# Value blocks projected in the attention's output banks, and the reciprocal rms row fetched by two DMAs

## What is computed

```python
# layer 0, 8 heads of 64 channels
hn = group_norm(x, gn1_scale, gn1_bias)                       # 32 groups
q, k, v = split(einsum('bchw,oc->bohw', hn, w_qkv) + b_qkv)   # per head
wgt = softmax(einsum('bct,bcs->bts', q * scale, k * scale))   # 1024 x 1024
a = einsum('bts,bcs->bct', wgt, v)
x = x + group_norm(einsum('bchw,oc->bohw', a, w_proj) + b_proj, gn2_scale, gn2_bias)
# layer 1, one head of 512 channels
qkv = einsum('oc,bcn->bon', w_qkv, x)            # weight-normed
rms = sqrt(mean(square(qkv), axis=1, keepdims=True)) + 0.0001
q, k, v = split(qkv / rms, 3, axis=1)
attn = softmax(einsum('bci,bcj->bij', q, k) * C ** -0.5)
h = einsum('bij,bcj->bci', attn, v)
out = (x + einsum('oc,bcn->bon', w_out, h)) * 2 ** -0.5
```

## Time and profile before

| | |
|---|---|
| runs | 3520.0, 3522.6, 3522.65 us |
| profiled execution | 3520.63 us |
| its span | 3518.8 us |
| TensorE's mean granted clock | 0.999 of full speed |

### The profile page before, as it was taken

The page is one execution under the profiler, slowest core; times in us unless marked ns, Lnnn a source line. Parts: engine busy times, 40 slices in busy tenths (PEclk is TensorE's granted clock), DMA queues, the critical chain, the costliest instruction groups (busy, mean ns, idle before and its releaser), DMA issues.

```text
span 3518.8 us, 52658 instructions
## 1 busy us (share of the span) xinstructions
PE 3457.8 (98%) x17360; PEld 2832.2 (80%) x17360; DVE 2077.7 (59%) x3388; ACT 1826.7 (52%) x3074; POOL 1086.0 (31%) x947
## 2 busy tenths in 40 slices
PE   7999999999999999999999999999999999999999
PEld 4788888878888788887878878788787887888878
DVE  4677436773378634786347854488444884457742
ACT  3677226862278522784237832388223882247822
POOL 0344203441045410453104531145211452124521
PEclk9999999999999999999999999999999999999999
DMA  8522214312234113331143220342213422142210
GB/s 312 156 53 61 92 54 127 85 37 84 82 99 97 66 43 103 89 86 72 37 121 89 68 84 34 112 97 61 84 37 110 95 61 84 43 137 62 61 48 24
DMA packets 63519, 294.41 MB, mean 84 GB/s; under 512 B 9200, under 2 KB 9456, under 8 KB 52464
## 3 DMA queue, kind: packets, MB, share of 16 engines
q1 hardware_dynamic: 63216, 290.65, 28.0%
HBM read 158.49 MB, written 31.46 MB: 54 GB/s over the span
## 4 chain that ended last, share of the span: by engine, by line
PE 85%; issue 6%; DVE 3%; ACT 2%; DMA 2%; POOL 2%; SPq 0%; ACTq 0%; DVEq 0%; POOLq 0%
PE big L430 28%; PE tps L529 14%; PE big L556 12%; PE ops L542 12%; PE ops L702 10%; PE big L626 6%; PE ops L430 1%; DVE XA L1252 1%; ACT PB L828 1%; PE big L594 1%; DMA d_m<-PT 1%; DMA d_u<-ST 1%; POOL XA L968 1%; DVE HL L1257 0%; DVE small L1180 0%
## 5 line engine op out<-in xcount | busy, mean ns | idle before, releaser
L958 POOL TENSOR_SCALAR PB<-PB,small 128x1024 f32<-128x1024 f32 x576 | 650.2, 1129 | 1304.4 <-DVE small L1186 1293.6
L834 ACT ACTIVATE PT<-tps 128x512 fp32r<-128x512 f32 x1088 | 601.7, 597 | 250.9 <-PE tps L529 247.8
L1191 DVE TENSOR_TENSOR PT<-tps,PT 128x512 fp32r<-128x512 f32 x1088 | 693.8, 679 | 39.0 <-ACT PT L834 38.6
L1180 DVE TENSOR_REDUCE small<-big 128x1 f32<-128x1024 f32 x512 | 625.1, 1221 | 63.7 <-PE big L556 60.3
L529 PEld LDWEIGHTS tps<-ident,PB 128*128 128x128 f32 x4608 | 526.8, 140 | 125.5 <-DVE PT L1191 56.2
L529 PE MATMUL tps<-ident,PB 128*128 128x128 f32 x4608 | 618.0, 275 | 9.0 <-DVE PT L1191 6.1
L828 ACT ACTIVATE PB<-big,small 128x1024 f32<-128x1024 f32 x512 | 572.6, 1118 | 74.3 <-DVE small L1180 71.3
L542 PE MATMUL ops<-PT,VT 128*128 128x512 f32 x2048 | 599.2, 414 | 0.0
L556 PE MATMUL big<-ST 128*128 128x512 f32 x2048 | 555.0, 393 | 12.3 <-ACT PB L828 11.2
L556 PEld LDWEIGHTS big<-ST 128*128 128x128 f32 x2048 | 381.9, 188 | 103.2 <-ACT PB L828 19.8
L542 PEld LDWEIGHTS ops<-PT,VT 128*128 128x128 f32 x2048 | 346.1, 189 | 47.4 <-DVE PT L1191 5.0
(11 more groups left out here) (158 smaller groups left out, 4652.2 us busy)
## 6 DMA issues: line engine op xcount, KB each, us to landing
ST<-ST SPq DMA_DIRECT2D x384, 256.0 KB, 5.0
W<-d_qk SPq DMA_DIRECT2D x32, 1024.0 KB, 5.3
XA<-in_x SPq DMA_DIRECT2D x8, 2048.0 KB, 7.7
X<-in_x SPq DMA_DIRECT2D x8, 2048.0 KB, 10.5
W<-d_wp SPq DMA_DIRECT2D x8, 2048.0 KB, 11.6
W<-d_g SPq DMA_DIRECT2D x8, 2048.0 KB, 11.9
W<-d_m SPq DMA_DIRECT2D x8, 2048.0 KB, 7.9
W<-d_u SPq DMA_DIRECT2D x8, 2048.0 KB, 10.2
```

The source lines that it names most:

```text
L834: act_fn(pt_slot(u, s)[:, 0, :], tps[n % 2][:], ACT.Copy).then_inc(s_pt_hi, 1)
L958: nc.gpsimd.tensor_scalar(PB[:, i, :], PB[:, i, :], rinv[:, i:i + 1], 1.0, ALU.mult, ALU.mult)\
L1180: V.tensor_reduce(negmax[:, i:i + 1], tile(("s", 4 * u + tb))[:], axis=AX.X, op=ALU.max, negate=True).then_inc(s_row_max, 1)
L1191: V.tensor_tensor(pt_slot(u, s)[:, 1, :], tps[n % 2][:], pt_slot(u, s)[:, 0, :].bitcast(f32), ALU.subtract).then_inc(s_pt_ready, 1)
```

## The change

Two things are changed. The value blocks 4 to 7 are all projected in the `ops` banks, one in each of the attention steps 0 to 3; two `big` tiles instead of three are filled with values ahead of the attention. Blocks 6 and 7 use the banks of blocks 4 and 5 again and wait for VectorE to have read these. The low parts of the four blocks are made by VectorE one step later each, as before.

The reciprocal row is no longer made by TensorE. `rcol` is stored by SP into a DRAM tensor of 1024 numbers, element by element in position order, SP waits for that store, and loads the row from there into RB with all 128 partitions reading the same 4 KB. Both come in SP's queue after the load of W for the value products and ahead of the wait for `("y", 3)`. The identity products, the ones product and the copy are gone, and ScalarE waits for `rcol` itself.

```diff
 def last_values(step):
-    return {0: NT - 2, 3: NT - 1}.get(step)
+    return {0: 4, 1: 5, 2: 6, 3: 7}.get(step)
...
-BIG = [("qk", j) for j in range(4)] + [("v", i) for i in range(3)]
+BIG = [("qk", j) for j in range(4)] + [("v", i) for i in range(2)]
...
-BIG += [("y", 0), ("y", 1), ("y", 2), ("y", 3), ("u", 0), ("u", 1), ("u", 2), ("r", 0)]
+BIG += [("y", 0), ("y", 1), ("y", 2), ("y", 3), ("u", 0), ("u", 1), ("u", 2)]
...
+        d_r = nc.dram_tensor("d_r", [N], f32)
...
-                sp.wait_ge(s_v_full, b * 2 + 2)
+                sp.wait_ge(s_v_full, b * 4 + 4)
...
                 sp.dma_start(W[0][:].bitcast(f32), d_u[:]).then_inc(s_ld_u, 16)
+                sp.wait_ge(s_r_col, b + 1)
+                own_wait(sp)
+                sp.dma_start(d_r.ap().rearrange("(s p) -> p s", p=P), rcol, allow_slow_non_contiguous=True)\
+                  .then_inc(s_r_stored, 16)
+                sp.wait_ge(s_r_stored, b * 16 + 16)
+                own_wait(sp)
+                sp.dma_start(RB[:], d_r.ap().partition_broadcast(P)).then_inc(s_r_row, 16)
...
                 def project_last_v(s):
-                    if s == NT - 2:
+                    if s == 4:
                         pe.wait_ge(s_y_out, b * 8 + CREDIT)
+                    if s >= 6:
+                        pe.wait_ge(s_v_ready, b * 6 + s - 3)
...
-                for i in range(3):
+                for i in range(2):
                     project_v(i)
...
-                t = released(("r", 0))
-                pe.wait_ge(s_diag_ready, b + 1)
-                for half in range(2):
-                    cols = slice(HALF * half, HALF * half + HALF)
-                    last = mm(t[:, cols], ones[:], PB[:, 0, cols], start=True, stop=True)
-                last.then_inc(s_big_full, 1)
...
-                act.wait_ge(s_diag_ready, b + 1)
+                act.wait_ge(s_r_col, b + 1)
...
-                link(V.reciprocal(rcol, rms))
-                for s in range(NT):
-                    last = V.tensor_scalar(PB[:, 0, P * s:P * s + P], ident[:], rcol[:, s:s + 1], None, ALU.mult)
-                last.then_inc(s_diag_ready, 1)
+                V.reciprocal(rcol, rms).then_inc(s_r_col, 1)
...
-                dve.wait_ge(s_big_full, at(("r", 0)))
-                V.tensor_copy(RB[:], tile(("r", 0))[:]).then_inc(s_r_ready, 1)
...
-                        dve.wait_ge(s_r_ready, b + 1)
+                        dve.wait_ge(s_r_row, b * 16 + 16)
```

More of the change, by code:

```diff
@@ L74 @@
 BIG_BASE = SETUP_BIG
-DVE_LINKS = 18
+DVE_LINKS = 17
 SCALE0 = float(CH) ** -0.5
@@ L244, in build @@
         s_rms_done = sem("rms_done")
-        s_diag_ready = sem("diag_ready")
-        s_r_ready = sem("r_ready")
+        s_r_col = sem("r_col")
+        s_r_stored = sem("r_stored")
+        s_r_row = sem("r_row")
         s_y_ready = sem("y_ready")
@@ L486, in released @@
                         kind, k = (BIG_LAST if last_batch else BIG)[i - 2]
-                        reader, per = {"v": (s_v_ready, 5), "qk": (s_nat_ready, 16), "s": (s_exp_done, 72),
+                        reader, per = {"v": (s_v_ready, 6), "qk": (s_nat_ready, 16), "s": (s_exp_done, 72),
                                        "proj": (s_pr_ready, 4), "gna": (s_gn_var, GN_PER_BATCH),
                                        "gnb": (s_gn_veps, GN_PER_BATCH),
-                                       "g": (s_prod_ready, 4), "r": (s_r_ready, 1),
+                                       "g": (s_prod_ready, 4),
                                        "y": (s_y_ready, 4), "u": (s_vp_ready, 8), "s1": (s_s1_ready, 8)}[kind]
@@ L536, in values0 @@
                         if u == 0:
-                            pe.wait_ge(s_v_ready, b * 5 + 5)
+                            pe.wait_ge(s_v_ready, b * 6 + 6)
                         elif u > 1:
@@ L809, in last_v_hi @@
                 def last_v_hi(s):
-                    act.wait_ge(s_v_full, b * 2 + s - 5)
+                    act.wait_ge(s_v_full, b * 4 + s - 3)
                     act_fn(v_heads(s, s + 1)[:, :, 0:4:3, :], ops[s % 2][:].rearrange("p (q x d) -> p q x d", x=2, d=CH),
@@ L1162, in last_v_lo @@
                 def last_v_lo(s):
-                    dve.wait_ge(s_v_hi, b * 2 + s - 5)
+                    dve.wait_ge(s_v_hi, b * 4 + s - 3)
                     v = v_heads(s, s + 1)
```

## The result

The changed kernel takes 3500.6 us (median; 3499.7 to 3503.7 over four runs), the kernel before 3522.4 us in the runs beside it. The ratio is 0.9942, with a 95% interval of 0.9928 to 0.9957: 21.8 us less in the medians. The forecast was 3504.4 us. Between the two profiled executions, which are what the forecast's sum was made from, 19.2 us went (3501.4 against 3520.6), where the sum said 18.2.

What follows compares the result with a forecast made beforehand. TensorE, busy in 98% of the span, was taken as the bound. Terms -15.2 (row), -8.1 (early scores), +3.5 (batch 0) and +1.6 (clock) gave -18.2 us: 3504.4 us from the 3522.6 median, range 3499 to 3514.

Steps and rivals of the forecast that it cites:

- the forecast's sum: Whole kernel: -15.2 for the row, -8.1 for values, +3.5 and +1.6 in batch 0, together -18.2 us.
- The row's price: TensorE between value products u2 and u4: removing the ones product saves 1.90 us a batch, 15.2 us in all.
- the bank's wait: Before value product u3: a 0.68 us wait for a bank, included in the row's 1.90 us, would go.
- The two DMAs: Row's store and load on SP: together 4 to 31.5 us, taken as about 10, at no path cost.
- 35.6 us of cover: Time from when the reciprocal's store can go out to the first scaled maximum, which reads the row first.
- The early scores: Attention step 0 starts after 0.66 us idle for the sixth stacking copy; seven batches gain 1.16 us each, 8.1 us.
- the lead: Step 4 starts 1.16 us earlier, at 543.84 instead of 545.00, in seven batches.
- Batch 0: Late sixth copy leaves TensorE idle 6.5 us before step 0: +3.5 us, and +1.6 us for a slow clock.
- the two slow pieces: Stretches behind the 1.8 us idle time ahead of gram products, where the clock fell: 1.57 us each, two of eight batches.
- The rival of five or more slow pieces: Clock falls behind the idle time ahead of gram products in most batches: 3510 to 3514 us; chance 0.15.
- The third rival: Element store outlasts its cover, the scaled maximum waits, each microsecond costs eight: 3611 us at 0.6 us a piece; chance 0.03.
- The point of decision: Store and load together beyond 35.6 us delay the maximum; from 37.9 us on the kernel is slower than before.

Runs made afterwards that it cites:

- filled kernels: Seven unread matmuls a batch added in TensorE's idle time ahead of the third gram product: kernel before 3516.4, values only 3513.2, full change 3498.4 us.
- early copies: Full change, with the second pair's weight load behind the first head's six copies and its query copies sent before the key products: 3495.3 us.
- early copies with the matmuls: Kernel with the query copies sent early, plus seven unread matmuls a batch ahead of the third gram product: 3489.2 us.
- old kernel with the matmuls: Kernel before the change, plus seven unread matmuls a batch ahead of the third gram product: 3516.4 us.
- late row: Full change, with the row's store and load held back on SP until the last value product is full: 3567.7 us, ratio 1.0133.

## Why the prediction was right, and where its working was not

**The row's price.** Forecast 1.90 us a batch, measured 2.03 between batches of the kernel with the row alone, 1.90 between u2 and u4 (7.34 to 5.44), and 1.77 by the filled kernels with the 0.13 of the bank to add. The share of the bank's wait, which I put into the 1.90 without a number of its own, is 0.13 us; the 0.68 us idle time of the weight loads in the earlier trace rows was mostly hidden under the ones product. Right.

**The two DMAs.** The store was between the bounds, 9.2 us median and 11.7 in batch 0 (385.89 to 397.62), where I had taken 10 us for store and load together; with the load's 5.8 they make 15 to 17.5 us. Both lie within the 35.6 us of cover. The load behind them on SP went out at 398.13 and nobody waited for it. The Trainium skill's rule ("DMA: Bandwidth & Descriptors", "Rules for kernel authors": one descriptor per element) agrees with this trace: the packet counts above have one small packet for each number, and the 4 KB took over four times as long as a store of 256 KB. It cost nothing, since the end did not depend on it. One sentence of the prediction was wrong: the trace before did have pieces under 512 B. The load of `vec`, 48 floats on each of 128 partitions and so 192 B a piece, landed in 4.3 us:

```profile
vec<-in_vecs SPq DMA_DIRECT2D x1, 24.0 KB, 4.3
```

It would not have changed the sum.

**The early scores.** The wait for the sixth copy came where the sum put it: 0.4 to 0.5 us of idle time and a late start of step 0 in seven batches. I wrote 0.66, which counts from the time at which the last matmul could have been followed by the next. Steps 0 to 4 take 14.64 us, forecast 14.63; the lead is 1.19 us in the one stretch of the kernel with the values alone and 1.15 - 0.13 = 1.02 in the filled kernels, forecast 1.16. TensorE has no wait in steps 1 to 4.

**Batch 0.** Forecast +3.5 us, idle time 6.5 us, and +1.6 for the clock. In the changed kernel's first execution step 4 starts 121.60 - 105.13 = 16.47 us after step 0, 5.3 more than before (11.13); TensorE was idle for 6.9 us. So 5.1 forecast and 5.3 measured. The clock did fall there, in all six executions that hold this idle time (5.6 to 7.1 us); steps 0 to 4 took 15.96 to 17.18 us in them, so that it cost 1.3 to 2.6 us over the 14.63. With the 2.6 us of the early copies it fell too and cost 1.4 us (16.01), and with the 0.7 us of the early copies with the matmuls it did not fall (14.63). The 1.09 us that TensorE waited here in the kernel before, which the sum took as given, is chance: two executions that keep values ahead of the scores, the old kernel with the matmuls and the one with the row alone, have no such wait.

**The clock elsewhere.** I had left the two slow pieces of the profiled execution in the sum and given the range their place. The changed kernel had one, 1.6 us less, and that was luck. It explains why the sum was 1.0 us short (3502.4 forecast for the like of the profiled execution, 3501.4 measured): 1.6 for the slow piece and 0.8 for slightly larger gains a batch on the one side, 1.2 for a later step 0 in batch 0 (105.13 against 103.92; 104.03 in the second execution, so that this too is chance) and 0.2 in batch 0's steps on the other. Against the median of the runs the forecast was 3.8 us too high, and 3500.6 lies 1.6 us above the low end of the range; no step of the sum accounts for that. The rival of five or more slow pieces did not come in the changed kernel, but what it names is real: the kernel with only the values moved had six. The step that was thin is the one that took a rival for small because two of eight had fallen: the number was another one after nearly every edit. Why isn't shown; that it goes with the length of a batch is a guess.

**The third rival's price.** "Each microsecond costs eight" was wrong in its working. In the late row the maximum waited 13.4 us where 4.2 are usual, so it was 9.2 us late, and TensorE stood 5.35 us: the second score tile took up the rest. The slow clock behind the wait then cost some 2.5 us more, so that a batch grew by 7.6 us for 9.2 us of lateness, less than one for one. The point of decision was therefore put somewhat early; it did not matter, as the cover was never used up.

**Parts against the whole.** By the medians the row alone brings 13.2 us and the values alone 1.0, together 14.2, where both bring 19.3. Read so, the parts seem to help each other. The batch lengths say otherwise: 2.03 and 1.19 make 3.22, and both together took 3.16 off (429.70 to 426.54 in the mean). The difference is the number of slow pieces: four and six in the profiled executions of the parts, one in the whole. The runs as a whole agree by their mean granted clock: 0.9976 and 0.9966 in the parts, 0.9980 in the whole.

What stays open: why the clock falls in some batches and not in others behind the same idle time, and why the medians of the first comparison lie 2.6 us further apart than the profiled executions and 3.7 further than the filled kernels.

## What to carry to other kernels

Where one engine is busy in 98% of the span, price an edit by the distance between two starts on that engine on both sides of it, and ask of work that is moved which hidden wait stood behind it: here a copy with 5 us of lead became the wait as soon as 5.4 us of matmuls left its front. Compare two versions by the length of an undisturbed batch as well as by the median; a clock that falls in one to six batches was worth 1.6 to 9.6 us here, as much as a part of the edit. Two us of idle time ahead of dense work can be cheap to fill and dear to leave.

## What the runs showed of the hardware

Behind the 1.8 us idle time the granted clock fell in 1 to 6 of 8 batches (2 in the kernel before, 1 and 1 in the two executions of the changed one, 4 with the row alone, 6 with the values alone, 4 with the early copies, 3 with the late row), each time at a cost of 1.6 us. Where the idle time was filled down to 0.3 us, it fell there in none of 32 batches of four kernels. The Trainium skill ("TensorE: Matmul & The Clock Gate", Part 1) says that idle time puts the clock to half. These executions agree, and show it for an idle time shorter than the page asks for, under 2 us. By the medians, matmuls that nobody reads bought 4.6 us in the old kernel, 7.4 in the one with the values alone, 6.1 in the one with the early copies (luck in batch 0 may be part of this) and 4.0 in the changed one.

A store of 1024 single floats from 128 partitions lands in 8.4 to 9.2 us (medians of eight, in seven executions; once 11.7 us). By my estimate that is 0.13 to 0.14 us for each of the 64 pieces of a DMA engine, where a piece of 4 KB took 0.33 in the load of X.
